# A fused two-layer kernel on one core: orders in attention, an unrolled normalizing stage, register reads and the token list moved

## The reference

```
x = x + tanh(g_xattn[0]) * cross_attention(layernorm(x), ctx)        # 16 heads of 16
x = x + tanh(g_ffn[0])   * recurrent_mixture(layernorm(x))
x = x + tanh(g_xattn[1]) * alignment(ctx, layernorm(x))              # dynamic time warping
x = x + tanh(g_ffn[1])   * capacity_experts(layernorm(x))            # top 1 of 8

# recurrent_mixture(h): a GRU of width 1024 = 8 experts x 128 routes the tokens
h0  = h.mean(axis=1) @ ctx_w.T + ctx_b ;  xw = h @ gru_w_ih.T
r,z = sigmoid(xr + hr), sigmoid(xz + hz) ;  n = tanh(xn + r * hn)    # hw = state @ gru_w_hh.T
state = (1 - z) * n + z * state                                      # 100 steps
score = (1 - cos(h @ expr_w.T, state)) * (1 + penalty)               # per token and expert
out   = sum over the 2 best experts of share * mlp_e(h)  +  shared_mlp(h)
```

## Time and profile before

| | us |
|---|---|
| three runs, median (lowest, highest) | 3427.74 (3424.08, 3431.61) |
| the profiled execution, its own time | 3427.98 |
| its span | 3426.4 |
| TensorE busy in it | 2984.2 (87%) |
| VectorE, ScalarE, GpSimd busy | 1428.4, 961.3, 814.7 |
| mean granted TensorE clock | 0.942 of full |

### The profile page before, as it was taken

How to read it: one execution, slowest core, us unless ns; L and a number is a source line. 1 busy time by engine, 2 the same in 40 slices (tenths; PEclk the granted TensorE clock), 3 DMA queues, 4 the chain that set the end, 5 groups by cost and what they waited for, 6 DMA issues and landing times. The chain is left out here.

```text
span 3426.4 us, 72405 instructions
## 1 busy us (share of the span) xinstructions
PE 2984.2 (87%) x27712; PEld 1663.2 (49%) x27713; DVE 1428.4 (42%) x3112; ACT 961.3 (28%) x2547; POOL 814.7 (24%) x770
## 2 busy tenths in 40 slices
PE   5999999976999999999999999999899977008698
PEld 3666666642444444444444444468555545006454
DVE  4666666654232333232323232354222236996311
ACT  2555555542111111111111111121122226562111
POOL 1111111100122222222222222243344422004243
PEclk9999999986999999999999999999999989558699
DMA  6000000003000000000000000041122244105143
GB/s 220 23 22 22 22 18 22 22 10 123 17 23 17 23 17 23 17 23 17 23 17 23 17 23 17 23 186 39 38 41 42 42 107 118 44 0 185 51 112 73
DMA packets 81214, 163.00 MB, mean 48 GB/s; under 512 B 12056, under 2 KB 54936, under 8 KB 76408
## 3 DMA queue, kind: packets, MB, share of 16 engines
q1 hardware_dynamic: 56472, 106.67, 10.0%
q0 software_dynamic: 21360, 37.53, 5.1%
q10 hardware_dynamic: 3184, 15.86, 1.2%
HBM read 119.63 MB, written 40.37 MB: 47 GB/s over the span
## 5 line engine op out<-in xcount | busy, mean ns | idle before, releaser
L909 PE MATMUL gru_ps_rz<-whh,scratch 128*32 128x512 f32 x6400 | 707.4, 594 | 0.0
L675 POOL TENSOR_TENSOR scratch<-scratch 128x1024 f32<-128x1024 f32 (+3 forms) x246 | 369.5, 1527 | 818.6 <-DVE stat L689 656.3
L909 PEld LDWEIGHTS gru_ps_rz<-whh,scratch 128*32 128x32 f32 x6400 | 197.8, 110 | 451.9 <-issue 451.9
L914 PE MATMUL gru_ps_n<-whh,scratch 128*32 128x256 f32 x6400 | 363.7, 379 | 0.0
L841 DVE TENSOR_TENSOR scratch<-scratch,gru_state 128x256 f32<-128x256 f32 x100 | 52.2, 522 | 661.1 <-ACT scratch L870 661.1
L524 PE MATMUL att_turned<-ident,att_probs 100*121 100x100 f32 x1536 | 271.7, 286 | 31.1 <-ACT att_probs L357 25.1
L914 PEld LDWEIGHTS gru_ps_n<-whh,scratch 128*32 128x32 f32 x6400 | 208.1, 110 | 179.9 <-issue 59.8
L524 PEld LDWEIGHTS att_turned<-ident,att_probs 100*121 100x121 f32 x1536 | 211.7, 185 | 164.3 <-issue 130.3
L428 DVE TENSOR_REDUCE att_neg_max<-att_score 100x1 f32<-100x361 f32 x512 | 248.2, 526 | 57.8 <-PE att_score L516 57.8
L357 ACT ACTIVATE att_probs<-att_score,att_neg_max 100x361 f32<-100x361 f32 x512 | 261.3, 569 | 9.8 <-DVE att_neg_max L428 9.8
L870 ACT ACTIVATE scratch<-gru_ps_rz 128x512 f32<-128x512 f32 x100 | 59.7, 597 | 720.0 <-PE gru_ps_rz L909 720.0
(11 more groups left out here) (369 smaller groups left out, 4352.2 us busy)
## 6 DMA issues: line engine op xcount, KB each, us to landing
table<-in_w SPq DMA_DIRECT2D x16, 1024.0 KB, 6.9
states<-gru_state SPq DMA_DIRECT2D x100, 128.0 KB
scratch<-states SPq DMA_DIRECT2D x25, 512.0 KB, 3.6
whh<-in_whhT POOLq DMA_DIRECT2D x8, 1536.0 KB, 17.6
att_c_in<-in_ctxT SPq DMA_DIRECT2D x32, 363.0 KB, 3.0
dist_ctx<-in_ctxT SPq DMA_DIRECT2D x32, 363.0 KB, 6.1
align_ctx<-in_ctx_rows SPq DMA_DIRECT2D x32, 363.0 KB
whh<-in_guT ACTq DMA_DIRECT2D x8, 1024.0 KB, 11.7
```

The source lines that it names most:

```text
L675: done = nc.gpsimd.tensor_tensor(last.prod[:, row:row + rows, :], a, b, ALU.mult)
L909: last = nc.tensor.matmul(ps_rz[quarter(q), :], stateT[c % 2][:, quarter(c // 2)], rz_columns(whh, c, q), start=False, stop=(c == GC - 1))
L914: last = nc.tensor.matmul(ps_n[quarter(q), 0:GQ], stateT[c % 2][:, quarter(c // 2)], n_columns(whh, c, q), start=(c == 0), stop=(c == GC - 1))
```

## The change

Four edits.

1. Attention. `outputs(b, u, 0)` stands ahead of `turn_probs(b, 4)`. On ScalarE, heads with h % 4 == 1 take their exponential first and the odd copy after it. The statistics of the rows for the next normalization are taken here: VectorE writes the sum to `x1[u]`, and copies it to the rows at h = 12, where it also takes bn_stats; bn_aggr follows at h = 13 and a copy of mean and variance at h = 14. POOL's store waits for the copy.
2. Between attention and the recurrence. The block `row_statistics` of x1 is gone, `normalized_rows_out` is unrolled with eight buffers and eight PSUM banks, and it also does what the first block of `gru` did: the loads (wih on POOL's queue; wc, the bias and the gate on ScalarE's), the initial state, and the sum over steps, which ScalarE now takes as the accumulator output of two copies of 128 x 100 a batch. `we` is loaded by SP at the start of the recurrence, and TensorE waits for it in its first step.
3. Routed tiles. Of the three register reads of a loop turn one stays at its head, one stands behind the gate products and one behind the up products of the first tile.
4. Token list. The parts of a piece are spread over LISTED[j] - 3 to LISTED[j] - 1, the routing pieces end by step 29, and `rows_listed` and `factor` are written in step 50, ahead of the last shared sums.

```
# attention, TensorE / ScalarE / VectorE
                 for h in range(HEADS):
+                    if h == FIRST_OUTPUTS:          # FIRST_OUTPUTS, OUTPUTS = 4, {8: 1, 12: 2}
+                        outputs(b, u, 0)
                     turn_probs(b, h)
...
-                    if h % 2 == 1:
-                        act.wait_ge(t_psum, HEADS * b + h + 1)
-                        at_least(act, o_psum, HG * b + h // 4 - 1)
-                        nc.scalar.copy(probsT[...], turned[1][0:KC, 0:3 * S]).then_inc(odd_ready, 1)
+                    if h % 4 == 3:
+                        odd_out(b, h)
                     for r in EXPONENTIALS[h % 4]:
                         head = head_at(b, u, h - h % 4 + r, last)
                         if head:
                             exponential(*head)
+                    if h % 4 == 1:
+                        odd_out(b, h)
...
+            def keep_output(b, u):
+                dve.wait_ge(x1_ready, b + 1)
+                at_least(dve, aggregated, b)
+                nc.vector.tensor_scalar(rows_of(b), x1[u][:], 1.0, None, ALU.mult).then_inc(x1_kept, 1)
+                nc.vector.bn_stats(stats[:], x1[u][:]).then_inc(stats_done, 1)
# normalized_rows_out, unrolled (RING, BANKS = 8, 8)
+        def _(pool):
+            pool.dma_start(wih[:], wihT).then_inc(wih_in, 16)
...
+            for b in range(B):
+                if b >= RING:
+                    dve.wait_ge(h_stored[b % RING], 16 * (b // RING))
+                    dve.wait_ge(h_turned, b - RING + 1)
+                v.tensor_scalar(h[b % RING][:], rows[:, b, :], mean_var[:, b, 0:1], rstd[:, b:b + 1], ...)
...
+            act.dma_start(wc[:], wcT).then_inc(wc_in, 16)
+            for q in range(4):
+                act.dma_start(cb[32 * q:32 * q + 32, :], ctx_b[...].partition_broadcast(32)).then_inc(cb_in, 16)
+            act.dma_start(gate[:, :], g_ffn.partition_broadcast(P)).then_inc(gate_in, 16)
+            act.wait_ge(eps_added, 1)
+            nc.scalar.activation(rstd[:], rstd[:], ACT.Sqrt).then_inc(root_ready, 1)
+            for b in range(B):
+                act.wait_ge(h_turned, b + 1)
+                for k in range(KT):
+                    nc.scalar.activation(hT[:, k, :, b], turned[b % BANKS][:, k * S:(k + 1) * S], ACT.Copy,
+                                         accum_out=x_sum[:, k, b:b + 1]).then_inc(hT_ready, 1)
# gru
+            sp.dma_start(we[:], weT).then_inc(we_in, 16)
+                    if j == 0:
+                        pe.wait_ge(we_in, 16)
# mixture: token list
                 for j, at in enumerate(LISTED):
-                    if at - 2 <= i <= at:
-                        for _ in range(1 if i == at else 2):
+                    if at - 3 <= i < at:
+                        for _ in range(1 if i == at - 1 else 2):
                             next(listing[j], None)
...
+                if i == LISTED[-1] + 2:
+                    dve.wait_ge(piece_done, len(PIECES))
+                    v.tensor_scalar(rows_listed[:], ...).then_inc(listed, 1)
+                    v.tensor_copy(factor[:], ...).then_inc(listed, 1)
# mixture: routed tiles
+            def turn_of(n, u, here, before=None, after=None):
...
                 up(ps_g[u], 0, here, u).then_inc(g_done, 1)
+                e_before = expert_of(n - 1) if before is True else before
...
                 up(ps_u[u], 1, here, u).then_inc(u_done, 1)
+                e_after = expert_of(n + 1) if after else None
...
             def two_tiles(i):
+                here = expert_of(2 * i - 1)
+                after = turn_of(2 * i - 1, 1, here, before=True, after=True)
+                turn_of(2 * i, 0, after, before=here, after=False)
```

More of the change, by code:

```diff
@@ L135, in _ @@
         @block.vector
         def _(dve):
[L137 to L144, removed]
+            v = nc.vector
+            v.tensor_scalar(rstd[:], mean_var[:, :, 1], LN_EPS, None, ALU.add).then_inc(eps_added, 1)
@@ L146, in _ @@
+            dve.wait_ge(first_psum, 1)
+            v.scalar_tensor_tensor(state[:], turned[0][:, 0:GQ], 1.0 / S, cb[:], ALU.mult, ALU.add).then_inc(first_ready, 1)
+            dve.wait_ge(first_ready, 1)
         @block.tensor
         def _(pe):
[L148 to L155, removed]
@@ L157, in _ @@
-            repeat(pe, B // AT_ONCE, turn_of)
+            for b in range(B):
+                pe.wait_ge(h_ready, b + 1)
+                if b >= BANKS:
+                    pe.wait_ge(hT_ready, KT * (b - BANKS + 1))
+                for k in range(KT):
+                    last = nc.tensor.transpose(turned[b % BANKS][:, k * S:(k + 1) * S], h[b % RING][:, k * P:(k + 1) * P], ident[0:S, 0:S])
+                last.then_inc(h_turned, 1)
+            pe.wait_ge(wc_in, 16)
+            pe.wait_ge(hT_ready, KT * B)
@@ L159, in _ @@
+            for q in range(4):
+                for k in range(KT):
+                    last = nc.tensor.matmul(turned[0][32 * q:32 * q + 32, 0:GQ], x_sum[:, k, :], wc[:, k, q * GQ:(q + 1) * GQ],
+                                            start=(k == 0), stop=(k == KT - 1))
+            last.then_inc(first_psum, 1)
         @block.scalar
         def _(act):
[L161 to L166, removed]
@@ L184, in constants @@
+            act.wait_ge(gate_in, 16)
+            nc.scalar.activation(gate[:, :], gate[:, :], ACT.Tanh).then_inc(gate_out, 1)
+            act.wait_ge(gate_out, 1)
 def constants(nc, pool, filled, ident, one_row):
@@ L468, in turn_of @@
                         divide(b - 1)
+                    if h == OUTPUT + 2 and not first:
+                        statistics_taken(b - 1)
                     if h in VALUES and not last:
@@ L802, in turn_of @@
                              states[bass.ds(it, 1)].rearrange("a j b n -> (a j b) n")).then_inc(routed_in, 16)
+            sp.dma_start(we[:], weT).then_inc(we_in, 16)
+            for tile, source in shared_sources:
+                sp.dma_start(tile, source).then_inc(last.shared_in, 16)
             repeat(sp, TILES, turn_of)
@@ L1577, in _ @@
             turn_x(0, 0, 16)
-            turn_of(0, 0, None, expert_of(0), first=True)
+            turn_of(0, 0, expert_of(0), after=False)
             two_tiles(1)
@@ L1581, in _ @@
                 two_tiles(i)
-            before, here, after = expert_of(N - 3), expert_of(N - 2), expert_of(N - 1)
-            turn_of(N - 2, 1, before, here)
-            turn_of(N - 1, 0, here, after, last=True)
+            here = expert_of(N - 2)
+            after = turn_of(N - 2, 1, here, before=True, after=True)
+            turn_of(N - 1, 0, after, before=here)
             turn_mid(N - 1, 0)
```

194 lines of the change are left out of this document (92 added, 102 removed).

## The result

The changed kernel takes 3349.4 us (median of 4 runs, 3348.4 to 3356.2) against 3429.7 of the kernel before (median of 4): 0.9762 of its time, 95% interval 0.9748 to 0.9776, so 77 to 86 us faster. The forecast was 3351 us and a gain of 77. The profiled execution of the changed kernel is its slowest one (3356.15, span 3354.5), and the two spans differ by only 71.9 us.

The account below looks back on a forecast made before the run. TensorE was taken to bound the kernel, so its standing still counts: attention 11, middle 27, list 15 and 2, routed tiles 22 sum to 77, and 3427.98 - 77 = 3351 us. Forecast 3340 to 3358, range 3337 to 3380.

Parts of the forecast that it names:

- Attention, 11 us: Attention's order edits bring the scores of heads 8 to 11 forward 0.36 us a batch, 11 us in 30 batches.
- the second edit now counts: Attention, ScalarE's swap: exponential 7 starts at 388.75 instead of 389.12, so the scores go at about 389.38 instead of 389.74.
- VectorE's additions, 0: Attention: four more VectorE operations a batch, about 1.1 us, charged nothing behind maximum 15; up to 35 us if uncovered.
- Middle, 27 us: Between attention and recurrence: 10 + 4 + 14 - 1 = 27 us saved, bounds 14 and 33.
- First tile: Middle: the first normalized tile comes at about 766.9 instead of 776.9, 10 us saved.
- start of the recurrence: Middle, from the loop to the first recurrence matmul: 4.7 us left of 18.8, so 14 saved.
- loop: Middle's 32 normalized tiles: 0.5 to 0.6 us a tile on ScalarE, 20 us taken, 4 saved, bounds 16 and 31.
- The wait for the expert weights: Start of the recurrence: TensorE newly waits for expert input weights issued by SP, put at 1 us.
- Rival (1): Middle: DMA engines bound it, stores wait behind 4 MB, loop 31 us, middle saves 14 instead of 27: 3364; chance 0.15.
- List, 15 and 1.7 us: Token list beside the shared expert: pieces one step earlier save 15 us, bounds 7 and 18; first gather's wait saves 1.7.
- Routed tiles, 22 us: Routed loop: two register loads moved off the head, turn 11.64 us instead of 12.51, 22 us saved over 26 turns.
- the cover: Routed tiles: TensorE's sequencer runs some 1.7 us ahead, which with four matmuls of 0.43 us hides the moved register loads.

Follow-up runs that it names:

- experiment 8: Three more unread bn_stats of 100x256 a batch on VectorE, added to the changed kernel: 3371.5 us, ratio 0.9835, period 22.131.
- experiment 11: Two more unused reads of the expert number ahead of a turn's first middle product, added to the changed kernel: 3346.6 us, ratio 0.9754.

## Why the prediction was right

- **Attention, 11 us.** Right in size, by a wrong step, and so by luck. The period fell by 0.315 instead of 0.36, some 9.8 us in 31 batches. The failed step is "the second edit now counts: ScalarE takes exponential 7 ahead of odd copy 5, at 388.75 instead of 389.12". 389.12 was the order of before, with the product between the two turns; by my own times head 5 is turned right behind head 4 at about 387.6, which lets the copy end before the maximum. The swap then moves next to nothing (21.520 and 21.500), and the exponential came at 3.35 us behind head 3's turn, not 3.27, because maximum 7 slipped by 0.2 and not by 0.1.
- **VectorE's additions, 0.** Right: 0.003 us a batch, and experiment 8 shows that it ends within the next 0.99 us of work.
- **Middle, 27 us.** Measured 27.3. First tile 9.8 us earlier (10 forecast), start of the recurrence 14.6 (14), loop 2.9 (4). Two small terms failed. The wait for the expert weights (1 us) did not come: SP issues them at 785.88, 0.7 us ahead of the first gate matmul, they land in 4.9 us, and the expert product at 791.10 follows without a gap. And the loop's length has another cause than the one I gave: ScalarE needs 0.46 us a tile, a little below my 0.5 to 0.6, and eight buffers did not cover the 6.24 us for which a store waits behind the weights. Rival (1)'s mechanism is there, with a loop of 21.4 us instead of its 31. That the 20 came so near is luck: the faster ScalarE made up for a wait that the sum did not hold. No kernel with the middle's change alone was timed; its total stands on the trace.
- **List, 15 and 1.7 us.** Measured 18.5. The idle left is 2.1 (1.4 taken), the busy time 12.4 instead of the 12.1 of an undisturbed rate, and the gather's wait 1.03 instead of 2.4. From the routing score to the gather TensorE's busy time fell from 120.7 to 113.0 us, with the granted clock up from 0.94 to 1.00; 5.1 of that are the list's own matmuls, and 2.6 are others behind the stalls, where I took 1. The term was mis-sized low by 2 us.
- **Routed tiles, 22 us.** Measured 22.4 to 22.6 with period 11.64, as worked out; experiment 11 shows the cover to be larger than I counted.
- **The total.** By medians the gain is 80.3, by the profiled pair 71.9. The forecast of 77 from one profiled execution lies between them. Attention by its periods and the other three stages add up to 78. The list's 2 us too little and attention's 1 too much partly cancel.

## What to carry to other kernels

Two order edits that aim at one wait need not add (0.30 and 0.39 us alone, 0.32 together): list for each which instruction comes last at the wait once the other edit is in, with the new times of everything between, not the old ones. Work on a second engine was free until its idle time at that place was used up (0.003 us for the first four operations, 0.63 for the next 0.99 us), so measure the room before adding the next instruction. A load moved beside stores can hand its time to whoever waits for these stores; taking the ring away gave back 2.1 of 6.24 us and moved the rest to the end of the block. Whether fewer bytes there, or stores that go faster than 238 GB/s, would remove it was not run.

## Hardware behaviour that I had not expected

- Copying 100 columns on ScalarE with accumulation and reading the accumulator takes 0.23 us in steady state (starts 762.26, 762.49, 762.72 in the changed kernel; 0.46 a tile of two), where 256 columns took 0.30 to the next start and the read 0.10.
- Register loads on TensorE's sequencer take 0.30 us each by their rows, 0.75 us apart at the loop's head and 0.65 us apart in its middle.
- After the weights have landed, the stores of 100 KB follow each other at 239 GB/s at a DMA share of 0.69 (770 to 781 us), against 132 GB/s in the loop of before, which waited for its ring of four.
- With 3 MB from POOL's queue under way, the first of eight stores of 100 KB from SP's landed only with the load's end (769.8, and the load by 769.4), and the stores then moved 238 GB/s at a DMA share of 0.68, where the stretch with the load had 346 GB/s at 0.93.
